# Mixture-of-experts tail of an attention kernel: tokens and expert weights turned by DMA, last projection in quarters, reordered experts

## The chip, the cores and the metric

The kernel runs on one core of one Trainium2 chip. The time is device microseconds (us) for one execution. A core has TensorE (PE), VectorE (DVE), ScalarE (ACT), GpSimd (POOL) and SyncE (SP), which here issues every DMA. Each engine works through its own list of instructions in order and waits on semaphores for the others.

## The reference

```python
h = layernorm(x)                          # x: 8 sequences x 128 tokens x 256
q, k, v = h @ wq, h @ wk, h @ wv          # 16 query heads, 4 key/value heads of 128
q, k = rope(rms_norm(q)), rope(rms_norm(k))
k_ctx, v_ctx = rms_norm(ctx @ wk_ctx), ctx @ wv_ctx
p = softmax(q @ [k_ctx; k].T / sqrt(128) + causal)
x = x + (p @ [v_ctx; v]) @ wo
t = layernorm(x)                          # 1024 tokens x 256
score = sigmoid(t @ gate.T)               # 8 experts, the two best by score + bias
for e in range(8):                        # bf16 products
    xe = bf16(t * score_of_e_or_0)
    out += (silu(xe @ w1[e].T) * (xe @ w3[e].T)) @ w2[e].T
out += (silu(t @ sh_w1.T) * (t @ sh_w3.T)) @ sh_w2.T
x = x + out
```

The shapes are fixed: 8 sequences of 128 tokens, model width 256, expert width 128, context of 128 rows for each sequence.

## The kernel before

The attention part runs sequence by sequence. A "row" is one sequence `b`, and each row has four groups `g` of four query heads. Rows 0 and 7 are written out and rows 1 to 6 are a loop. Within a row PE computes the scores, turns the query of the next group and the probabilities (`turn_probs`), mixes the values (`mix`), and projects the queries two groups ahead. The output projection `out_proj(b - 1)` (L1314) of 48 matmuls into `proj[0]` stands in the next row. The matmuls are done on split high and low parts, so ACT makes a high part (`o_copy`, `p_copy`, all through the helper at L435) and DVE the low part (`o_low`, `p_low`, at L879).

After row 7 comes the mixture of experts. The 1024 tokens are two halves `n` of four tiles of 128 tokens, and step `k` of 16 is expert `k % 8` on half `k // 8`. The order of all instructions is written out by hand.

- The weights of the experts are loaded in rows 0 to 3, cast to bf16 by POOL (L815, the signals `w1_cast`, `w3_cast`, `w2_cast`), and turned by PE in `turn_experts` (L1328): six groups of eight 128x128 transposes into PSUM, copied to SBUF by ACT or DVE (`turned`). The shared expert's weights are turned as four fp32 transposes (L1447).
- The normalised tokens `xn2_all` are turned in pairs of tiles (`turn_xn2`, L1346) and copied to `xn2T` (`xn_copy`). The router is `logits` (L1355) on PE, `gate_exp` on ACT (L622) and ten small DVE instructions (`router`, L1077), which end in `weight`.
- For each step `k`, DVE scales two of the four token tiles by `weight` and POOL the other two (`e_scale`, L1102 and L825) into `xb`, which has two buffers. PE turns the eight blocks (`turn_tokens`, L1458, line L1469) into `turn` or `o_ps`, and ACT copies them to `xbT` (`e_copy`). `expert_up` (L1473, L1481) makes the two hidden products, ACT the SiLU (`e_act`, L647), DVE the product (`e_hidden`, L1115), and `expert_down` (L1485, L1488) adds into `proj`. Steps k and k + 1 use two sets of PSUM banks, so `expert_up(k)` waits for `e_hidden(k - 2)`, and PE runs `expert_up(k + 1)` ahead of `expert_down(k)`.
- The shared expert is `shared_up` (L1493, L1501), a SiLU (L655), a product (L1134) and `shared_down` (L1505), which first clears the two banks with a product with zeros (L1512) and then makes eight passes of fp32 matmuls (L1516).
- PE's order around the tail: `logits(0)`, `turn_probs(8, 0)`, shared weights, w3, tokens of tiles 4 and 5, the last `mix`, w2, the whole of `out_proj(7)`, `shared_up(0)`, `turn_xn2(3)`, `turn_tokens(0)`, `logits(1)`, and only then the experts.
- DVE after row 7: the low parts, the ten instructions of `router(0)`, a weight copy (L979), `e_scale(0)` and `e_scale(1)`, then `residual(7)` (L961) and `second_norm(7)` (L972), whose root POOL makes between its own `e_scale` instructions (`l2_root`, L714).
- SP's list: the loads, `next_ctx(b)` (L408: the context of the next sequence, as soon as its buffer is free), w3 after `w1_cast` (L417), w2 after `w3_cast` (L420), and the four stores of the output (L427).

## Time and profile before

| | |
|---|---|
| time, median of 3 runs | 376.64 us (376.41 to 376.70) |
| time of the profiled execution | 377.97 us |
| its span, first to last instruction | 376.3 us |
| PE busy | 343.7 us, 91% |
| DVE busy | 325.6 us, 87% |
| ACT busy | 271.2 us, 72% |
| POOL busy | 165.8 us, 44% |
| mean granted clock of PE | 0.977 |

The span is what the trace covers; the time of an execution lies a little above it. Busy shares are averages over stages with different limits, and overlapped matmuls count as busy. PE's clock is given as a share of its full 2.4 GHz. Of the span, roughly the last 60 us belong to the mixture of experts, with the output projection of row 7 among them.

### The profile page before, as it was taken

Reading aid. Unit: us, or ns where it says so; the run is one execution under the profiler, and the core shown is the slowest. Engines: PE = TensorE matmul, PEld = TensorE weight load, DVE = VectorE, ACT = ScalarE, POOL = GpSimd, SP = SyncE. Lnnn points to the kernel's source line nnn. Section 1 sums busy time; section 2 is a strip of 40 time slices with the busy share of each in tenths; the row PEclk is TensorE's granted clock in tenths of the full one; section 3 lists DMA queues with packets and bytes.
Section 4 is the critical chain, followed back from the end, with each engine's and each line's share of the span. In section 5 each row is a group of like instructions: output and inputs, shape, how many; then the busy total and the mean of one; then the engine's idle time right before and its main releaser. Section 6 shows DMA issues by size and latency. Waiting matters only on the chain.

```text
span 376.3 us, 7781 instructions
## 1 busy us (share of the span) xinstructions
PE 343.7 (91%) x2471; PEld 237.3 (63%) x2476; DVE 325.6 (87%) x625; ACT 271.2 (72%) x913; POOL 165.8 (44%) x242
## 2 busy tenths in 40 slices
PE   6697798799999999999999999999999999998994
PEld 5373555376567665866685577567666778674572
DVE  1668999998999899899989998999899897759653
ACT  3557879676986797699759876986797567167562
POOL 3356565652754275427344443644174300334330
PEclk9788989999999999999999999999999999989999
DMA  5967000000030003000000000000000000000011
GB/s 179 379 212 223 17 0 2 1 2 14 3 111 0 14 0 111 14 1 0 0 14 0 0 0 14 0 0 0 0 0 1 2 0 2 2 0 3 22 35 57
DMA packets 11603, 13.49 MB, mean 36 GB/s; under 512 B 824, under 2 KB 9024, under 8 KB 11584
## 3 DMA queue, kind: packets, MB, share of 16 engines
q1 hardware_dynamic: 11584, 13.25, 11.0%
q8 instruction: 10, 0.16, 0.2%
q14 instruction: 9, 0.07, 0.1%
HBM read 12.20 MB, written 1.05 MB: 35 GB/s over the span
## 4 chain that ended last, share of the span: by engine, by line
PE 40%; DVE 24%; ACT 17%; issue 10%; POOL 4%; DMA 2%; SPq 1%; DVEq 1%; ACTq 0%; POOLq 0%
PE proj L1324 10%; ACT probs L524 8%; PE pt_ps L1300 5%; DVE probs L953 5%; PE proj L1157 4%; PE turn L1246 3%; DVE nmax L941 3%; DVE pT_lo L879 3%; PE o_ps L1310 3%; POOL q_rot L744 3%; PE sc_ps L1267 2%; ACT pT_hi L435 2%; DMA wq<-in_L_xattn_wq_dram 2%; ACT q_junk L468 2%; DVE q_t L870 2%
## 5 line engine op out<-in xcount | busy, mean ns | idle before, releaser
L524 ACT ACTIVATE probs<-sc_ps,nbias,q_r 128x256 f32<-128x256 f32 x128 | 70.8, 574 | 2.8 <-DVE nbias L945 2.8
L744 POOL TENSOR_TENSOR q_rot<-q_t 128x512 f32<-128x512 f32 x32 | 41.4, 1295 | 42.8 <-DVE q_t L872 42.0
L953 DVE TENSOR_SCALAR probs<-probs,rden 128x256 f32<-128x256 f32 x128 | 51.2, 461 | 1.1
L1157 PE MATMUL proj<-wq_hi,xT 128*128 128x512 f16 x128 | 40.1, 396 | 2.9 <-DVE wq_lo L863 2.9
L435 ACT ACTIVATE pT_hi<-pt_ps 128x512 f16<-128x512 f32 x64 | 34.8, 597 | 10.9 <-PE pt_ps L1300 10.9
L468 ACT ACTIVATE q_junk<-proj 128x128 bf16<-128x128 f32 x128 | 34.0, 295 | 11.7 <-DVE q_t L872 11.7
L879 DVE SCALAR_TENSOR_TENSOR pT_lo<-pt_ps,pT_hi 128x512 f16<-128x512 f32 x64 | 41.0, 682 | 0.6 <-ACT pT_hi L435 0.6
L941 DVE TENSOR_REDUCE nmax<-sc_ps 128x4 f32<-128x1024 f32 x32 | 38.9, 1214 | 1.5 <-PE sc_ps L1289 1.5
L831 POOL TENSOR_TENSOR wq<-xn_all,weight 128x512 bf16<-128x512 f32 x16 | 17.1, 1074 | 44.1 <-DVE weight L1098 23.4
L1324 PE MATMUL proj<-wo_hi,oT_hi 128*128 128x256 f16 x128 | 34.9, 273 | 0.0
L1324 PE MATMUL proj<-wo_lo,oT_hi 128*128 128x256 f16 x128 | 34.9, 273 | 0.0
L1324 PE MATMUL proj<-wo_hi,oT_lo 128*128 128x256 f16 x128 | 34.9, 273 | 0.0
L1300 PE MATMUL pt_ps<-ident,probs 128*128 128x128 f32 x256 | 34.2, 278 | 0.3
L701 POOL TENSOR_TENSOR q_r<-q_me,power 128x4 f32<-128x4 f32 x32 | 33.3, 1042 | 2.5
L435 ACT ACTIVATE qT_hi<-turn 128x512 f16<-128x512 f32 x32 | 19.5, 610 | 19.9 <-PE turn L1246 19.9
L1300 PEld LDWEIGHTS pt_ps<-ident,probs 128*128 128x128 f32 x256 | 29.5, 143 | 0.8 <-DVE probs L953 0.5
L1246 PE MATMUL turn<-ident,q_rot 128*128 128x128 f32 x128 | 19.8, 277 | 10.6 <-POOL q_rot L744 4.9
L468 ACT ACTIVATION_READ_ACCUMULATOR q_junk<-proj 128x1 f32 x128 | 28.5, 227 | 0.0
L524 ACT ACTIVATION_READ_ACCUMULATOR probs<-sc_ps,nbias,q_r 128x1 f32 x128 | 27.6, 215 | 0.0
L1310 PE MATMUL o_ps<-pT_hi,v_hi 128*128 128x512 f16 x64 | 24.3, 379 | 3.2 <-DVE pT_lo L879 3.2
L879 DVE SCALAR_TENSOR_TENSOR oT_lo<-o_ps,oT_hi 128x512 f16<-128x512 f32 x32 | 21.9, 686 | 5.8 <-ACT oT_hi L435 5.8
L1267 PE MATMUL sc_ps<-kT_hi,qT_hi 128*128 128x256 f16 x128 | 24.5, 273 | 0.5 <-ACT probs L524 0.2
(216 smaller groups left out, 920.7 us busy)
## 6 DMA issues: line engine op xcount, KB each, us to landing
wq<-in_L_xattn_wq_dram SPq DMA_DIRECT2D x4, 512.0 KB, 9.1
w<-in_L_ffn_w_dram SPq DMA_DIRECT2D x2, 1024.0 KB, 10.5
wq<-in_L_xattn_wo_dram SPq DMA_DIRECT2D x1, 2048.0 KB, 8.2
ctx_b<-in_ctx_dram SPq DMA_DIRECT2D x8, 128.0 KB, 2.1
out_dram<-x_all SPq DMA_DIRECT2D x4, 256.0 KB, 2.2
x_all<-in_x_dram SPq DMA_DIRECT2D x1, 896.0 KB, 12.3
wkc<-in_L_xattn_wk_ctx_dram SPq DMA_DIRECT2D x1, 512.0 KB, 4.2
wk<-in_L_xattn_wk_dram SPq DMA_DIRECT2D x1, 512.0 KB, 5.1
```

The lines of the kernel that those rows point to most:

```text
L435: return nc.scalar.activation(out_, in_, ACT.Copy, scale=scale)
L468: last = nc.scalar.activation(junk[:, head], bank[:, head], ACT.Square, scale=scale, accum_out=dst[:, h:h + 1])
L524: last = nc.scalar.activation(probs[:, h, :], sc_ps[:, h, :], ACT.Exp, bias=nbias[:, h:h + 1], scale=q_r[:, g, h:h + 1], accum_out=den[:, ...
L701: nc.gpsimd.tensor_tensor(r, me, power[:], ALU.pow).then_inc(root, 1)
L744: nc.gpsimd.tensor_tensor(q_rot[:], q_t1[:], q_t2[:], ALU.add).then_inc(q_added, 1)
L879: return nc.vector.scalar_tensor_tensor(out=lo, in0=src, scalar=scale, in1=hi, op0=ALU.mult, op1=ALU.subtract)
L941: nc.vector.tensor_reduce(nmax[:], sc_ps[:], AX_X, ALU.max, negate=True).then_inc(s_max, 1)
L953: last = nc.vector.tensor_scalar(probs[:, h, :], probs[:, h, :], rden[:, h:h + 1], None, ALU.mult)
L1157: last = nc.tensor.matmul(bank[:], xT[:, a, c, :], w[:, c, cols], start=(n == 0), stop=(n == 3 * DC - 1))
L1300: last = nc.tensor.transpose(pt_ps[:, a, h * P:(h + 1) * P], probs[:, h, a * P:(a + 1) * P], ident[:])
L1310: last = nc.tensor.matmul(o_ps[:], v[:, a, g * P:(g + 1) * P], p[:, a, :], start=(a == 0 and i == 0), stop=(a == 1 and i == 2))
L1324: last = nc.tensor.matmul(proj[0][:, 0:D], o[:, h // R, (h % R) * P:(h % R + 1) * P], w[:, h, :], start=(h == 0 and i == 0), stop=(h == H ...
```

## The change

1. The expert weights are turned by six DMAs of SP (`dma_start_transpose`, 256 KB each) in rows 1 to 4 in place of PE's 48 transposes and their six copies.
2. The scaled tokens are turned by one such DMA for each step `k` (256 KB, from SBUF to SBUF) in place of eight PE transposes and ACT's copy. The buffers are four (`xb`) and six (`xbT`). Of the four tiles ACT now scales one, DVE one and POOL two. DVE and ACT scale five steps ahead (`LEAD`).
3. `out_proj(7)` is cut in quarters by group; three run ahead of the last low part.
4. `logits(0)` goes into row 7, and the shared weights are turned there. DVE's `router(0)` goes around the last `p_low` and ahead of the last `o_low`. Two copies in row 7 and that of tiles 4 and 5 go from DVE to ACT.
5. `logits(1)`, its exponential and `router(1)` come after the first half's experts have begun.
6. The clearing products (L1512) go; the first shared product into each bank starts it.

```diff
--- before.py
+++ after.py
...
         hid_s = spare[:, 512:1024]
         silu_e = spare[:, 1024:2048].rearrange("p (a t) -> p a t", a=2)
-        xbT = spare[:, 2048:3072].bitcast(BF16).rearrange("p (a c t) -> p a c t", a=2, c=DC)
-        xb = spare[:, 3072:4096].bitcast(BF16).rearrange("p (a t d) -> p a t d", a=2, t=TT)
+        xb_homes = (spare[:, 3072:3584], spare[:, 3584:4096], k_sum[:], k_rot[:])
+        xbT_homes = (spare[:, 2048:2560], spare[:, 2560:3072], k_t1[:], k_t2[:], kc_n[:], q_t1[:])
+        xb = [h.bitcast(BF16).rearrange("p (c t d) -> p c t d", c=DC, t=TT) for h in xb_homes]
+        xbT = [h.bitcast(BF16).rearrange("p (c t) -> p c t", c=DC) for h in xbT_homes]
+        NB, NX = len(xb), len(xbT)
+        LEAD = 5
...
+        def token_turned(eng, k):
+            eng.wait_ge(d_xbT[k % NX], 16 * (k // NX + 1))
...
@@ -411,16 +414,38 @@
+            def turn_up(dst, src):
+                for half in half_e:
+                    sp.dma_start_transpose(dst[:, half].rearrange("p e c n -> p (e c) n"),
+                                           src[:, half].rearrange("p e d -> p (e d)")).then_inc(d_wT, 16)
+            def turn_down():
+                for half in half_e:
+                    sp.dma_start_transpose(w2T[:, half].rearrange("p e (c q) -> p (e c) q", c=DC),
+                                           w2_b[:, half].rearrange("p e c n -> p (e c n)")).then_inc(d_wT, 16)
             next_ctx(2)
             next_ctx(3)
             sp.wait_ge(w1_cast, 4)
             sp.dma_start(w1_32[:], w3.rearrange("e h d -> h e d")).then_inc(d_w3, 16)
+            turn_up(w1T, w1_b)
             next_ctx(4)
             sp.wait_ge(w3_cast, 4)
             sp.dma_start(w1_32[:].rearrange("p e (c h) -> p (e c) h", c=DC),
                          w2.rearrange("e (c p) h -> p (e c) h", p=P)).then_inc(d_w2, 16)
-            with sp.Fori(5, B) as b:
+            turn_up(w3T, w3_b)
+            next_ctx(5)
+            sp.wait_ge(w2_cast, 4)
+            turn_down()
+            with sp.Fori(6, B) as b:
                 next_ctx(b)
+            for k in range(E * NT):
+                for scaled in (e_scaled, e_scaled2, e_scaled3):
+                    sp.wait_ge(scaled, k + 1)
+                seen(sp, e_up, k - NX + 1)
+                sp.dma_start_transpose(xbT[k % NX].rearrange("p c (t n) -> p (c t) n", t=TT),
+                                       xb[k % NB].rearrange("p c t d -> p (c t d)")).then_inc(d_xbT[k % NX], 16)
             with sp.Fori(0, B // 2) as i:
                 sp.wait_ge(y_added, i + 1)
...
+                    if g == 2 and last:
+                        act.wait_ge(t_sh2, 1)
+                        copy(gateT[:].rearrange("p c e -> p (c e)"), proj[0][:, D:D + DC * E])
+                        copy(sh2T[:], proj[0][:, 0:D]).then_inc(r_sh2, 1)
+                        xn_copy(1)
                     if g == 0:
...
-            turned(w1T[:, half_e[0]], proj[0][:].bitcast(BF16), t_w1a, r_w1a)
-            gate_exp(0)
-            p_copy(G * B - 1)
-            turned(sh13T[:], turn[:], t_sh13, r_sh13, "p a c n -> p (a c n)")
-            turned(w3T[:, half_e[0]], proj[0][:].bitcast(BF16), t_w3a, r_w3a)
-            o_copy(G * B - 1, G - 1)
-            turned(w2T[:, half_e[0]], pt_ps[:, 0, :].bitcast(BF16), t_w2a, r_w2a, "p e n -> p (e n)")
...
+            def e_scale(k):
+                act.wait_ge(g_weight, k // E + 1)
+                if k >= NB:
+                    token_turned(act, k - NB)
+                dst, src, w = tile_of(k, 0)
+                copy(dst, src, w).then_inc(e_scaled3, 1)
...
-            xn_copy(3)
-            e_copy(0)
-            gate_exp(1)
+            o_copy(G * B - 2, G - 2)
+            gate_exp(0)
+            turned(sh13T[:], turn[:], t_sh13, r_sh13, "p a c n -> p (a c n)")
+            xn_copy(2)
+            p_copy(G * B - 1)
+            o_copy(G * B - 1, G - 1)
+            for k in range(LEAD):
+                e_scale(k)
             for n in range(NT):
                 act.wait_ge(sh_up, n + 1)
                 seen(act, sh_hid, n)
                 nc.scalar.activation(silu_s, shared_banks(n)[0], ACT.Silu).then_inc(sh_silu, 1)
                 if n == 0:
-                    e_copy(1)
+                    xn_copy(3)
                 e_act(E * n)
-                e_copy(E * n + 2)
+                if n == 0:
+                    e_act(1)
+                    gate_exp(1)
                 for k in range(E * n, E * (n + 1)):
-                    if k + 1 < E * (n + 1):
+                    if k + 1 < E * (n + 1) and k:
                         e_act(k + 1)
-                    if k + 3 < E * (n + 1) + (2 if n + 1 < NT else 0):
-                        e_copy(k + 3)
+                    if k + LEAD < E * NT:
+                        e_scale(k + LEAD)
...
-            e_scale(0)
-            e_scale(1)
+            for k in range(3):
+                e_scale(k)
             l2_root(B - 1)
-            for k in range(2, E):
+            for k in range(3, E):
                 e_scale(k)
...
-            p_low(G * B - 1)
-            turned(w3T[:, half_e[1]], proj[1][:].bitcast(BF16), t_w3b, r_w3b)
-            xn_copy(2)
-            o_low(G * B - 1, G - 1)
...
-            for part in range(4):
-                router(0, part)
-            turned(w2T[:, half_e[1]], sc_a.bitcast(BF16), t_w2b, r_w2b, "p e n -> p (e n)")
+            router(0, 0)
+            router(0, 1)
+            p_low(G * B - 1)
+            router(0, 2)
+            router(0, 3)
+            o_low(G * B - 1, G - 1)
             e_scale(0)
             e_scale(1)
             residual(B - 1)
+            e_scale(2)
             second_norm(B - 1)
-            e_scale(2)
+            e_scale(3)
+            e_scale(4)
...
-                if n == 0:
-                    e_scale(3)
                 for k in range(E * n, E * (n + 1)):
                     e_hidden(k)
-                    if k < 4:
+                    if k == 1:
+                        router(1, 0)
+                    if 1 <= k < 4:
                         router(1, k)
-                    if k + 4 < E * NT:
-                        e_scale(k + 4)
+                    if k + LEAD < E * NT:
+                        e_scale(k + LEAD)
...
+            def out_quarter(g):
+                if g == 0:
+                    pe.wait_ge(wo_low2, 1)
+                    pe.wait_ge(wo_low, 2)
+                    pe.wait_ge(r_sh2, 1)
+                pe.wait_ge(o_ready, G * (B - 1) + g + 1)
+                for h in range(g * R, (g + 1) * R):
+                    for i, (o, w) in enumerate(((oT_hi, wo_hi), (oT_hi, wo_lo), (oT_lo, wo_hi))):
+                        last = nc.tensor.matmul(proj[0][:, 0:D], o[:, g, (h % R) * P:(h % R + 1) * P], w[:, h, :],
+                                                start=(h == 0 and i == 0), stop=(h == H - 1 and i == 2))
...
                     if g == 2 and last:
                         turn_down_gate()
                         turn_xn2(0, (q_sq, G * B))
+                        turn_xn2(1, (q_ready, G * B))
                     if g == 3 and last:
-                        turn_xn2(1, (q_ready, G * B))
-                        pe.wait_ge(w1_cast, 4)
                         pe.wait_ge(r_sh2, 1)
-                        turn_experts(proj[0][:], w1_b, 0, False, t_w1a)
-                        pe.wait_ge(n_ready[0], 1)
-                        turn_experts(proj[1][:], w1_b, 1, False, t_w1b)
+                        logits(0)
+                        turn_shared()
...
-            logits(0)
+            turn_xn2(2, (s_exp, U))
+            out_quarter(0)
             turn_probs(B, 0)
...
-            turn_experts(proj[0][:], w3_b, 0, False, t_w3a)
-            pe.wait_ge(r_w1b, 1)
-            turn_experts(proj[1][:], w3_b, 1, False, t_w3b)
-            turn_xn2(2, (s_exp, U))
+            out_quarter(1)
             mix(U - 1, G - 1)
...
+            out_quarter(2)
+            out_quarter(3)
...
+            shared_up(0)
+            turn_xn2(3, (r_sh13, 1))
+            pe.wait_ge(d_wT, wT_landed)
             pe.wait_ge(n_ready[2], 1)
-            turn_experts(sc_a, w2_b, 1, True, t_w2b)
-            pe.wait_ge(r_w3a, 1)
-            out_proj(B - 1)
-            shared_up(0)
-            turn_xn2(3, (r_w2b, 1))
-            turn_tokens(0)
-            logits(1)
-            pe.wait_ge(r_w2a, 1)
             for n in range(NT):
                 expert_up(E * n)
-                if n == 0:
-                    turn_tokens(1)
-                turn_tokens(E * n + 2)
                 shared_down(n)
                 for k in range(E * n, E * (n + 1)):
                     if k + 1 < E * (n + 1):
                         expert_up(k + 1)
-                    if k + 3 < E * (n + 1) + (2 if n + 1 < NT else 0):
-                        turn_tokens(k + 3)
-                    if k + 1 == E * (n + 1) and n + 1 < NT:
+                    elif n + 1 < NT:
                         shared_up(n + 1)
+                    if k == 0:
+                        logits(1)
                     expert_down(k)
...
```

## Rows read from the trace of the kernel before

**Rows 1.** First line of the page: the profiled span.
```profile
span 376.3 us, 7781 instructions
```

**Rows 2.** Chain of waits, 316 to 371 us: start us, us, what.
```profile
316.27 1.31 PE o_ps L1310 x6
...
322.62 2.24 DVE wq L1108 x4
...
330.97 0.38 PE sc_ps L1481
...
351.08 1.72 PE sc_ps L1501 x4
...
360.67 0.43 PE sc_ps L1481 x2
...
361.53 0.45 PE turn L1469 x8
361.98 0.44 PE proj L1488 x4
...
369.86 0.60 ACT wq L647
```

**Rows 3.** PE in order of time: start us, us, what.
```profile
318.30 0.27 PE L1324 MATMUL proj<-wo_hi,oT_hi 128*128 128x256 f16 x1
...
323.54 1.88 PE L1501 MATMUL sc_ps<-xn2T,sh13T 128*128 128x512 f32 x4
...
327.57 0.63 PE L1351 MATMUL sc_ps<-ident,xn_all 128*128 128x128 f32 x4 [0.43 <-DVE xn_all L974]
...
328.97 1.92 PE L1360 MATMUL o_ps<-gateT,xn2T 128*128 128x8 f32 x16 [0.33 <-ACT xn2T L435]
...
354.35 0.60 PE L1488 MATMUL proj<-w2T,wk 128*128 128x256 bf16 x4
...
360.07 0.60 PE L1488 MATMUL proj<-w2T,wk 128*128 128x256 bf16 x4
...
361.81 0.60 PE L1488 MATMUL proj<-w2T,wk 128*128 128x256 bf16 x4
...
371.23 0.61 PE L1488 MATMUL proj<-w2T,wk 128*128 128x256 bf16 x4 [0.69 <-DVE wk L1115]
```

**Rows 4.** Groups by shape, 300 to 377 us: busy us, mean ns.
```profile
L831 POOL TENSOR_TENSOR wq<-xn_all,weight 128x512 bf16<-128x512 f32 x16 | 17.1, 1074 | 44.1 <-DVE weight L1098 23.4 <-PE o_ps L1469 12.2 <-PE turn L1469 8.5
...
L1115 DVE TENSOR_TENSOR wk<-pt_ps,wq 128x512 bf16<-128x512 f32 x16 | 11.0, 687 | 8.0 <-ACT wq L647 8.0
```

**Rows 5.** Windows of 1 us; PEclk follows POOL's column.
```profile
331.00:332.00 1.00, 1.00 (x7) 0.60 (x7) 0.00 (x0) 0.98 (x2) 0.00 (x0) 0.78 0.00 0
332.00:333.00 1.00, 1.00 (x12) 1.00 (x11) 0.00 (x0) 0.99 (x3) 0.13 (x1) 0.50 0.00 0
...
334.00:335.00 1.00, 1.00 (x4) 0.81 (x3) 1.00 (x2) 1.00 (x2) 0.96 (x1) 0.52 0.00 0
```

**Rows 6.** DVE, then ACT, in order of time.
```profile
339.64 1.40 DVE L1108 TENSOR_SCALAR wq<-xn_all,weight 128x256 bf16<-128x256 f32 x2
...
331.15 1.28 ACT L655 ACT_TABLE_LOAD   x1
332.44 0.60 ACT L655 ACTIVATE wq<-sc_ps 128x512 f32<-128x512 f32 x1
```

**Rows 7.** Page, DMA issues: KB each, median us to landing.
```profile
wq<-in_L_xattn_wo_dram SPq DMA_DIRECT2D x1, 2048.0 KB, 8.2
ctx_b<-in_ctx_dram SPq DMA_DIRECT2D x8, 128.0 KB, 2.1
out_dram<-x_all SPq DMA_DIRECT2D x4, 256.0 KB, 2.2
```

**Rows 8.** SP's queue in order of time.
```profile
107.03 0.38 SPq L417 DMA_DIRECT2D w<-in_L_ffn_w_dram  x1
121.62 0.33 SPq L410 DMA_DIRECT2D ctx_b<-in_ctx_dram  x1
```

More of the change, by code:

```diff
@@ L222, in xattn_moe_kernel @@
         d_w2 = sem("d_w2")
+        d_wT = sem("d_wT")
         d_sh = sem("d_sh")
@@ L1043, in row @@
                         wo_split(1)
-                    if g == 3 and last:
-                        turned(w1T[:, half_e[1]], proj[1][:].bitcast(BF16), t_w1b, r_w1b)
                     if g == 2 and not last:
@@ L1326, in out_proj @@
                 last.then_inc(wo_done, 1)
-            def turn_experts(bank, src, half, per_chunk, signal):
-                for j in range(8):
-                    e, c = half * (E // 2) + j // DC, j % DC
-                    one = src[:, e, c, :] if per_chunk else src[:, e, c * P:(c + 1) * P]
-                    last = nc.tensor.transpose(bank.bitcast(BF16)[:, j * P:(j + 1) * P], one, identb[:])
-                last.then_inc(signal, 1)
             def turn_down_gate():
@@ L1344, in turn_down_gate, with turn_shared @@
                 last.then_inc(t_sh2, 1)
+            def turn_shared():
+                for a, src in enumerate((sh1, sh3)):
+                    for c in range(DC):
+                        last = nc.tensor.transpose(turn[:, (a * DC + c) * P:(a * DC + c + 1) * P],
+                                                   src[:, c * P:(c + 1) * P], ident[:])
+                last.then_inc(t_sh13, 1)
             def turn_xn2(i, free):
```

114 lines of the change are left out of this document (31 added, 83 removed).

## The prediction

> **What bounds the kernel now.** The span of the profiled execution is 376.3 us [rows 1]. It ran in 377.97 us, 1.67 more, and the median of the runs shown is 376.64, 0.34 above the span. I make the sum on the span and add 0.34. The edit leaves rows 0 to 6 alone but for SP's list, so I read the chain of waits and PE's order from 316 us on. The reader should see three stretches there. First, the last `mix`, begun at 316.27 [rows 2], is followed by the whole of `out_proj(7)`, from 318.30 to 323.54 [rows 3]: 48 matmuls in 5.24 us, 1.31 a quarter. Second, up to the first expert product at 330.97 [rows 2] stand `shared_up(0)` (two groups of 1.72 [rows 2]), a wait of DVE and POOL for the norm of tile 7, its transposes at 327.57 and `logits(1)` of 1.92 [rows 3]. Third, the experts run with PE as the bound: in the second half `expert_down` begins at 360.07 and 361.81 [rows 3], a step of 1.75 us that is 0.87 for `expert_up` (two of 0.43), 0.45 for the token transposes and 0.44 for `expert_down` [rows 2]. The clock fell to half (1.2 of 2.4 GHz) as these began [rows 5].
>
> **Weights by DMA.** PE loses six groups of eight transposes, of which the token group has the price, 0.45 [rows 2], so 2.7 us; two such groups (0.9) stand between the last `mix` and the projection. The six copies on ACT and DVE go with them. On SP each pair of DMAs stands ahead of `next_ctx`. Between SP's issues at 107.03 and 121.62 [rows 8] there are 14 us, and the context is wanted a row later still, so two DMAs of even 4 us cost nothing. If they took over 7 us each, SP would begin to run late, and the transpose DMA would be lost for the tokens long before that.
>
> **Last projection in quarters.** Ahead of the last `mix`, PE loses four groups of eight (1.8) and tiles 2 and 3 (0.44, now in group 2, under a wait of PE for `p_low`), and gains two quarters (2.6); `logits(0)` and the shared weights only swap places. The last `mix` thus comes some 0.3 later. Its low part was ready at 316.27 + 1.31 + 0.60 (ACT) + 0.69 (DVE) = 318.9 [rows 2, 4], and will be at 319.3 with the signals; the third quarter and two parts of DVE's router (1.6) fill the time. The last quarter ends at 319.3 + 1.31 = 320.7, against 323.54. Gain 2.8. Who waits for the moved router: `e_scale(0)`, by less than it gains, since `weight` comes at 318.7 and not 322.0.
>
> **Up to the first expert.** `shared_up(0)` ends at 324.15. The norm of tile 7 took 3.9 us from the end of the projection, with two `e_scale` of DVE (2.24 [rows 2]) in front. Now it has the same two, held up by POOL: DVE's scaling of two tiles at 339.64 took 1.40 [rows 6], at a time when POOL was in its own, against 1.12 for two in the run of four (2.24) of which half lay beside POOL, so DVE's SBUF work stands until POOL's instruction is over. POOL has a third `e_scale` of 1.07 [rows 4] ahead of its root. I take 4.4 us, so 325.1, and 0.45 of transposes: the first expert product begins at 325.6 instead of 330.97. That is 5.4 gained in all; 0.5 less if POOL delays DVE twice, 0.9 more if it never does. `turn_tokens(0)` and `logits(1)` are no longer in front.
>
> **First half.** Before, from 330.97 to the start of `expert_down(7)` at 354.35 [rows 3], 23.4 us. After: 8 x 0.87 + 7 x 0.44 + 1.8 (`shared_down`, without clearing) + 1.9 (`logits(1)`) + 3.44 (`shared_up(1)`) = 17.2 us of PE at the full clock. Waits come on top. PE ends `expert_up(0)` at 326.4, but DVE's `e_scale(3)` and `e_scale(4)`, each held until POOL is through with its own, end at 327.1 and the shared product (0.69) at 327.8: `shared_down(0)` waits 1.4. ACT is no later: `e_scale(4)` waits for the first token DMA (323.6), then 0.4, the load of SiLU's table 1.28 [rows 6] and the SiLU 0.6 make 325.9. Behind `e_act(1)` stands the router's exponential: with SiLU on both sides it needs up to two more loads, 2.6, and behind it are queued ACT's `e_scale(5)` and `e_act(2)`; on DVE, `router(1)` waits for it, ahead of `e_hidden(2)`. From the end of `expert_up(1)`: ACT ends `e_act(2)` after 0.6 + 1.28 + 0.2 + 0.4 + 1.28 + 0.5 = 4.3, DVE ends `e_hidden(2)` after 5.2; PE has 1.9 + 0.44 + 0.87 + 0.44 + 0.87 = 4.5 of work until it wants that. So the two loads cost 0.7, not 2.6, and the router's rest in DVE another 1.2 in steps 3 to 6. If the exponential is in SiLU's table the loads cost nothing and 0.3 comes back. Sum 17.2 + 1.4 + 1.9 = 20.5, gain 2.9. The tile that ACT now scales shows nowhere; I take 0.4, between DVE's 0.56 a tile (2.24 for four) and half of a SiLU of 0.60 over twice the columns [rows 2]; either end fits in a step of 1.31.
>
> The trace has the SiLU at 332.44, directly behind the load that began at 331.15 [rows 6]. The Trainium skill (ScalarE: Activation LUTs, What ACT_TABLE_LOAD costs) has 1.28 us too, but counts a drain of 1.38 for each switch to another set. By its figures `e_act(2)` would come 2.8 later and the time would be 371.4.
>
> **Clock.** In four windows from 331 to 335 the granted clock was 0.78, 0.50, 0.50 and 0.52 [rows 5] (the window at 333 is as that at 332), which took 1.7 us of full speed. It fell after PE had idled 0.43 and 0.33 us [rows 3] and then run `logits(1)` with 8 columns a product. The new order has longer waits (1.0 before the last tokens' transposes, 1.4 before `shared_down(0)`) and the same 8 columns behind them, so I count 1.7 again: the first half then gains 1.2.
>
> **Second half.** Steps lose five token groups after `shared_down(1)`, 2.25 us. PE's work is then 1.31 a step, but the two PSUM sets make a loop: `expert_up` to `expert_down` of one step is SiLU 0.60 [rows 2] + product 0.69 [rows 4] + signals, 1.5, so two steps take 1.31 + 1.5, 1.4 each. Six steps give back 0.8. Ahead of `shared_down(1)` the clearing product (0.4) goes, but its wait for DVE's two sums stays and DVE's shared product follows them: nothing. Gain 1.4. POOL's 1.07 a step [rows 4] fits.
>
> **Token DMA.** Sixteen DMAs of 256 KB on one queue. The trace has none of this kind. From below: the load of 2048 KB in 8.2 [rows 7] is 1.0 us for 256 KB. From above: two contexts of 128 KB at 2.1 each, one after the other, 4.2. A store of 256 KB landed in 2.2 [rows 7]. I take a pace of 1.5 and a landing 3 us after issue, near the store. The first is issued at 320.2 and wanted at 325.6. With a pace up to 2 nothing waits beyond what is counted; at 2.5 the span grows by 2 to 4, as the tokens of steps 13 to 15 come late.
>
> The Trainium skill has two answers. Advanced Engine Details and Errata (X-Bar Transpose (TRN2)) says that transpose DMAs are as fast as others, which agrees with my choice. VectorE: DVE Perf Modes (The three transpose paths) gives 1309 ns for one 128x128 block by DMA and advises TensorE where PSUM will do; eight such blocks one after the other would be 10.5 us a step and put the kernel beyond 480 us. No row here shows either.
>
> **Sum.** 376.3 - 2.8 - 2.6 - (2.9 - 1.7) - 1.4 = 368.3 by these rounded terms; with the median's 0.34, 368.6.
>
> **Rivals.**
> - The clock holds. For it: 3.4 us of full work (`shared_up(0)`) come right before. Against: the longer waits. The time is 1.7 less, 366.9. Chance 0.18.
> - Tokens land late: a pace of 2.2 to 3 us, or other waits between the engines (POOL holding up DVE, a second fall of the clock). Between the bounds above it is well possible. 371 to 376, say 373. Chance 0.10.
> - A switch of ACT's table costs more than its load. If each of the two new ones held ACT for as long again as the load, 2.6 us, all of it would be on the path, since PE already waits for `e_hidden(2)`: 371.2. Against it stands the SiLU right behind its load. Chance 0.04. (The skill's drain is this rival.)
> - Slower: the DMA's pace becomes the bound of all sixteen steps. The last token must land by 368.8, when `expert_up(15)` stood before, to be no slower: 320.2 + 3 + 15 x pace = 368.8 gives 3.04 us. At 4.2, the upper bound, it lands at 386.2, 17 us worse: 394. For it: no row shows data turned on the way, and each DMA here is small. Against: plain transfers of this size are below 3 us. It decides from a pace of 3.04 us, 86 GB/s. Chance 0.20. (The skill's figure for single blocks is this rival.)
> - The change doesn't do what it says: SP's three waits and the four buffers hold the scaling back so that PE waits as long as it turned before, and nothing moves. At a step of 1.75 in both halves and the first expert still behind the norm, 376.6. Chance 0.03.
>
> **Chances.** Forecast 0.45. Faster by over 0.2% (about what a measurement of this kernel can tell from no change): 0.45 + 0.18 + 0.10 + 0.04 = 0.77; same 0.03; slower 0.20. The range is 365.0 to 377.0: below by the norm that POOL never delays (0.9), a clock that holds (1.7) and a table that serves both functions (0.3), with 0.7 for my rounding; above by everything but the slow DMA.
>
> **What would show it.** The last L1324 quarter's matmuls ending near 320.7. The first L1481 product near 325.6. Three loads of ACT's table after 320 us in place of one. A clock of 0.5 for some 3 to 4 us soon after `logits(1)`. Steps of 1.3 to 1.45 in the second half, with `expert_up` released by DVE. DMA transposes landing less than 2 us apart. Wrong would be waits of L1481 for a DMA, SP busy for over 2 us an issue, or contexts landing late in rows 2 to 5.

## The result, and the profile after

| | before | after |
|---|---|---|
| median of four executions on one chip | 376.52 us (374.57 to 376.70) | 366.07 us (364.95 to 366.59) |
| span of the profiled execution | 376.3 us [rows 1] | 364.3 us (it ran in 366.01) |
| mean granted clock of PE | 0.977 | 0.989 |

The ratio is 0.9736, with a 95% interval of 0.9709 to 0.9763: the kernel is 2.6% faster, 2.5 us more than forecast and inside the range. The head of the page after, and PEclk in 40 slices:

```profile
span 364.3 us, 7426 instructions
...
PEclk9899989999999999999999999999999999999999
```

The change did what it says: 22 DMA transposes appear, and with them the packets under 512 B rise from 824 to 24056 by the pages. PE in order of time, after (start us, us, engine, line, operation, out<-in, count, and in brackets the idle time before and what ended it):

```profile
298.76 1.04 PE L1315 MATMUL pt_ps<-ident,probs 128*128 128x128 f32 x8
...
317.49 0.27 PE L1338 MATMUL proj<-wo_hi,oT_lo 128*128 128x256 f16 x1
317.60 1.88 PE L1503 MATMUL sc_ps<-xn2T,sh13T 128*128 128x512 f32 x4
...
321.31 0.63 PE L1378 MATMUL turn<-ident,xn_all 128*128 128x128 f32 x4
321.77 0.59 PE L1483 MATMUL sc_ps<-wq,w1T 128*128 128x512 bf16 x2
...
324.01 1.97 PE L1515 MATMUL proj<-sh2T,wq 128*128 128x256 f32 x8 [1.21 <-DVE wq L1149]
...
326.67 1.85 PE L1387 MATMUL o_ps<-gateT,xn2T 128*128 128x8 f32 x16
...
332.06 0.61 PE L1490 MATMUL proj<-w2T,wk 128*128 128x256 bf16 x4 [0.93 <-DVE wk L1129]
...
337.35 0.61 PE L1483 MATMUL sc_ps<-wq,w1T 128*128 128x512 bf16 x2 [1.35 <-DMA wq<-k_sum]
...
343.68 0.60 PE L1490 MATMUL proj<-w2T,wk 128*128 128x256 bf16 x4
...
356.37 0.61 PE L1490 MATMUL proj<-w2T,wk 128*128 128x256 bf16 x4
357.82 0.61 PE L1490 MATMUL proj<-w2T,wk 128*128 128x256 bf16 x4
359.26 0.61 PE L1490 MATMUL proj<-w2T,wk 128*128 128x256 bf16 x4 [0.82 <-DVE wk L1129]
```

The first row is `turn_probs(7, 1)`, 8 transposes that open the tail in every kernel here. In the trace of before it began at 301.77:

```profile
301.77 1.04 PE L1300 MATMUL pt_ps<-ident,probs 128*128 128x128 f32 x8
```

The order of work ahead of it is the same but for SP's list and one POOL `memset`, yet its start differs between the twelve traces (298.50 to 301.77), and between the two of one kernel (301.77 and 300.83 before, 298.76 and 300.33 after). Where I looked, the granted clock of the first 50 us differed too: in the window from 28 to 32 us it was 0.90 before and 1.00 after, from 44 to 48 us 1.00 and 0.67. So I compare the tail from that row on. The table gives each mark as time after it. The kernel after was run and traced a second time, as was the kernel before.

| us after the start of `turn_probs(7, 1)` | before | before, again | forecast | after | after, again |
|---|---|---|---|---|---|
| last matmul of the last projection begins | 21.66 | 21.66 | 18.9 | 18.73 | 18.74 |
| first expert product begins | 29.20 | 29.34 | 23.8 | 23.01 | 23.03 |
| `expert_down(7)` begins | 52.58 | 52.58 | 46.0 | 44.92 | 44.19 |
| last `expert_down` begins | 69.46 | 69.47 | 61.5 | 60.50 | 59.78 |

The tail gained 9.0 and 9.7 us against a forecast of 8.0. After the last `expert_down` both kernels need another 5.0 to 5.2 us. The rest of the 12.0 us between the two spans is the start: 3.0 in this pair, but 0.5 between the two repeats (300.83 and 300.33). The start moves by 0.9 and 1.6 us between two executions of one kernel, so whether the change moves it at all is open.

DVE after, from its `e_scale(0)` and `e_scale(1)` to the shared product, and below it POOL in the same stretch (columns as above):

```profile
316.14 1.51 DVE L1124 TENSOR_SCALAR wq<-xn_all,weight 128x256 bf16<-128x256 f32 x2
317.80 0.42 DVE L992 SCALAR_TENSOR_TENSOR x_all<-proj,x_all 128x256 f32<-128x256 f32 x1
...
320.04 1.12 DVE L1003 TENSOR_SCALAR xn_all<-x_all,ln_mv,ln_rs 128x256 f32<-128x256 f32 x1 [0.76 <-POOL ln_rs L722]
321.08 1.13 DVE L1124 TENSOR_SCALAR k_rot<-xn_all,weight 128x256 bf16<-128x256 f32 x1
322.13 1.13 DVE L1124 TENSOR_SCALAR wq<-xn_all,weight 128x256 bf16<-128x256 f32 x1
323.18 0.68 DVE L1149 TENSOR_TENSOR wq<-pt_ps,wq 128x512 f32<-128x512 f32 x1
```

```profile
319.97 1.04 POOL L859 TENSOR_TENSOR k_rot<-xn_all,weight 128x512 bf16<-128x512 f32 x1
320.97 2.14 POOL L859 TENSOR_TENSOR wq<-xn_all,weight 128x512 bf16<-128x512 f32 x2
```

Three DVE instructions take 1.12 or 1.13 us each. The first, the norm's scaling, takes 0.41 with POOL at rest (experiment 5), and an `e_scale` of DVE alone takes 0.32 to 0.35. The first ends at 321.16 and the last at 323.26, both 0.15 behind the end of a POOL `e_scale` (321.01, 323.11). That chain, and not PE, decides when `shared_down(0)` may begin.

ACT after, its three table loads and what follows each:

```profile
320.47 1.28 ACT L681 ACT_TABLE_LOAD   x1
321.76 0.60 ACT L681 ACTIVATE wq<-sc_ps 128x512 f32<-128x512 f32 x1
...
327.49 1.28 ACT L654 ACT_TABLE_LOAD   x1
328.78 0.20 ACT L654 ACTIVATE r_exp<-o_ps 128x32 f32<-128x32 f32 x1
...
329.39 1.28 ACT L668 ACT_TABLE_LOAD   x1
330.69 0.60 ACT L668 ACTIVATE wq<-sc_ps 128x512 f32<-128x512 f32 x1
```

SP's queue after (the time is how long the issuing instructions held SP), and the page's list of DMA issues (count, median us from issue to landing):

```profile
104.48 5.00 SPq L419 DMA_TRANSPOSE w1T<-w_b  x2
...
316.63 2.63 SPq L447 DMA_TRANSPOSE wq<-wq  x2
...
331.83 1.24 SPq L447 DMA_TRANSPOSE wq<-k_sum  x1
```

```profile
wq<-wq SPq DMA_TRANSPOSE x4, 3.3
w1T<-w_b SPq DMA_TRANSPOSE x2, 5.4
...
wq<-k_sum SPq DMA_TRANSPOSE x1, 5.5
wq<-k_rot SPq DMA_TRANSPOSE x1, 5.1
```

A transpose of 256 KB mostly holds SP for 1.23 to 1.34 us (that of step 7 held it for 2.54), where the issue of a plain DMA held it for 0.33 to 0.38 [rows 8], and by the page's medians it lands 3.0 to 3.4 us after issue, where a store of the same size took 2.2 [rows 7]. Two of the sixteen token DMAs, those of steps 6 and 7, landed late, after 5.5 and 5.1 us.

### The profile page after: what moved, and what is told of

It reads as the page before. It is cut to its first block, busy times and chain, and to the rows that moved or that the text cites. A ratio compares the mean times of both kernels' runs of the same rounds, so it can differ in the third digit from the quotient of the medians.

```text
span 364.3 us, 7426 instructions
## 1 busy us (share of the span) xinstructions
PE 329.9 (91%) x2296; PEld 223.4 (61%) x2296; DVE 316.9 (87%) x602; ACT 263.7 (72%) x916; POOL 166.5 (46%) x241
## 2 busy tenths in 40 slices
DMA packets 34835, 19.25 MB, mean 53 GB/s; under 512 B 24056, under 2 KB 32256, under 8 KB 34816
## 3 DMA queue, kind: packets, MB, share of 16 engines
q1 hardware_dynamic: 34816, 19.02, 20.6%
## 4 chain that ended last, share of the span: by engine, by line
PE 35%; DVE 24%; ACT 18%; issue 10%; POOL 6%; DMA 3%; SPq 1%; DVEq 1%; ACTq 0%; POOLq 0%
PE proj L1352 10%; ACT probs L549 7%; DVE probs L982 5%; PE pt_ps L1315 5%; PE turn L1261 3%; DVE nmax L970 3%; POOL q_rot L772 3%; PE o_ps L1325 3%; DVE pT_lo L908 3%; PE proj L1172 3%; PE sc_ps L1282 3%; ACT pT_hi L460 2%; DVE q_t L899 2%; ACT kc_junk L493 2%; DMA wq<-in_L_xattn_wq_dram 2%
## 5 line engine op out<-in xcount | busy, mean ns | idle before, releaser
L772 POOL TENSOR_TENSOR q_rot<-q_t 128x512 f32<-128x512 f32 x32 | 42.4, 1325 | 41.3 <-DVE q_t L901 40.5
L1172 PE MATMUL proj<-wq_hi,xT 128*128 128x512 f16 x128 | 39.2, 389 | 2.1 <-DVE wq_lo L892 2.1
L460 ACT ACTIVATE qT_hi<-turn 128x512 f16<-128x512 f32 x32 | 19.5, 610 | 20.5 <-PE turn L1261 20.5
L1352 PE MATMUL proj<-wo_hi,oT_hi 128*128 128x256 f16 x112 | 30.5, 273 | 0.0
L1352 PE MATMUL proj<-wo_lo,oT_hi 128*128 128x256 f16 x112 | 30.5, 273 | 0.0
L1352 PE MATMUL proj<-wo_hi,oT_lo 128*128 128x256 f16 x112 | 30.5, 273 | 0.0
L460 ACT ACTIVATE oT_hi<-o_ps 128x512 f16<-128x512 f32 x32 | 19.6, 613 | 7.8 <-PE o_ps L1325 7.8
```

Of the source, the lines that this page charges most:

```text
L460: return nc.scalar.activation(out_, in_, ACT.Copy, scale=scale)
L772: nc.gpsimd.tensor_tensor(q_rot[:], q_t1[:], q_t2[:], ALU.add).then_inc(q_added, 1)
L1172: last = nc.tensor.matmul(bank[:], xT[:, a, c, :], w[:, c, cols], start=(n == 0), stop=(n == 3 * DC - 1))
L1352: last = nc.tensor.matmul(proj[0][:, 0:D], o[:, h // R, (h % R) * P:(h % R + 1) * P], w[:, h, :], start=(h == 0 and i == 0), stop=(h == H ...
```

## The experiments

My theory: the gain comes from PE's path in four places, as in the table, and the token DMAs stay hidden. The rivals: the DMA's pace is near its limit; the clock and not the removed work explains the surplus; the quarters bring nothing of their own. Every ratio is to the kernel before on the same chip in the same session. Its median was 376.16 us for experiments 1 to 3, 376.56 for 5 to 7 and the repeat of the changed kernel, and 377.29 for 4, so the ratios compare more safely than the times. "Changed kernel" means its second run, 366.58 us, ratio 0.9739.

**1. The DMA's pace, two and three times.** Each token DMA is preceded by one or two more that turn the same data into memory no longer in use, and the consumers count all of them.

```diff
-            eng.wait_ge(d_xbT[k % NX], 16 * (k // NX + 1))
+            eng.wait_ge(d_xbT[k % NX], 32 * (k // NX + 1))
...
+                for i in range(1):
+                    sp.dma_start_transpose(again[i * NX + k % NX]...,
+                                           xb[k % NB]...).then_inc(d_xbT[k % NX], 16)
                 sp.dma_start_transpose(xbT[k % NX]...
```

> The changed kernel with each of the 16 token DMAs issued twice in a row (the extra one writes to unused memory, and the step waits for both), so that a step takes two issues of SP, 2.6 us in place of 1.3. Nothing of the result is left out. Theory A (the token DMAs are hidden up to a pace of about 2 us, the bound is PE and the loop of PSUM banks): the first tokens still land before they are wanted, the last ones late; 3 to 6 us slower than the changed kernel, 369 to 372 us. Theory B (the landing of the tokens already sets the pace of the changed kernel, as the one wait of 1.4 us at step 6 suggests): every step pays, 16 x 1.3 = 20 us, 386 us.

> As before with each token DMA issued three times: 3.9 us a step, beyond the point of 3.04 us from which the prediction called the change slower than the old kernel. Theory A: the DMA is then the bound of all steps; the last token lands at 317 + 3 + 15 x 3.9 = 378 us of the span and the end follows some 7 us later, 383 to 392 us, slower than before the change by 2 to 4%. If the buffers or other waits had hidden more, it would stay below 377.

Measured: with two 377.46 us, ratio 1.0018 (0.9993 to 1.0043); with three 398.64 us in two executions, ratio 1.0586 (1.0517 to 1.0656). SP's queue with two, then some of the waits of its PE from 316 us on (us in total, times, longest):

```profile
316.42 1.26 SPq L455 DMA_TRANSPOSE w<-wq  x1
317.73 1.33 SPq L457 DMA_TRANSPOSE wq<-wq  x1
319.17 1.26 SPq L455 DMA_TRANSPOSE w<-wq  x1
```

```profile
PE sc_ps L1493 <- DMA k_t<-k_rot: 2.4, 1, 2.4
```

A step costs 2.75 us with SP issuing for 2.59 of them (316.42 to 319.17), and 4.14 with three. PE waited for seven of the sixteen tokens, 9.6 us in all, and the whole gain was gone: slower than theory A allows, faster than B. With three it waited 24 us, and the time overshot what was expected. Most of that is the pace: over the fifteen steps from the first real token DMA (319.38) to the last (382.73) it was 4.22 and not 3.9, which makes 4.8 us, and the first one came 2.4 later than assumed. The clock also stood at 0.50 to 0.62 in three stretches of 4 to 12 us, but behind the first two PE caught up and was waiting for tokens again. So the slower rival's mechanism is real, and its place, the last `expert_up`, is right. Its point of decision was put at a pace of 3.04; the real tokens of the doubled kernel were issued from 317.73 to 360.82, 2.87 apart, and the last `expert_up` began at 365.37, which is 66.9 after `turn_probs(7, 1)` against 67.0 before. The limit is thus about 2.9, and the changed kernel, at 1.31, is far from it.

**2. The second router's logits ahead of the experts again.** `logits(1)`, its copy and its exponential go back to where before had them; all else is the changed kernel.

```diff
             pe.wait_ge(n_ready[2], 1)
+            logits(1)
             for n in range(NT):
...
                     elif n + 1 < NT:
                         shared_up(n + 1)
-                    if k == 0:
-                        logits(1)
                     expert_down(k)
```

> The changed kernel with logits(1) and its exponential back ahead of the experts, so that one load of the SiLU table follows the last exponential and the two further loads are gone. Theory A: 1.9 us of logits and a wait of 0.6 for the copy of xn2 come ahead of the first expert, SiLU and the shared product come 3 us later, and 1.9 us of PE work and about 0.9 of waiting at steps 2 and 3 go: 0 to 1 us slower, 366 to 367 us. Theory B (the two table loads of 1.28 us, or more with a drain, are all on the path): 1 to 3 us faster, 363 to 365 us.

Measured: 370.64 us, ratio 0.9843 (0.9806 to 0.9881), 4.1 above the changed kernel (3.9 by the ratios) and against both expectations. Its PE:

```profile
324.44 1.92 PE L1386 MATMUL o_ps<-gateT,xn2T 128*128 128x8 f32 x16 [0.78 <-ACT xn2T L460]
...
329.38 3.75 PE L1514 MATMUL proj<-sh2T,wq 128*128 128x256 f32 x8 [1.41 <-DVE wq L1148]
332.92 0.74 PE L1482 MATMUL sc_ps<-wq,w1T 128*128 128x512 bf16 x2
...
337.99 0.61 PE L1489 MATMUL proj<-w2T,wk 128*128 128x256 bf16 x4 [1.01 <-DVE wk L1128]
```

Windows of 4 us, first of this kernel, then of the changed kernel (PE, PEld, DVE, ACT and POOL busy with instructions, then PEclk, DMA share, GB/s):

```profile
324.00:328.00 4.00, 3.41 (x19) 2.20 (x20) 0.98 (x1) 1.87 (x4) 2.57 (x3) 0.80 0.68 131
328.00:332.00 4.00, 2.62 (x6) 2.19 (x7) 1.55 (x3) 1.00 (x2) 0.35 (x1) 0.50 0.00 0
```

```profile
324.00:328.00 4.00, 3.99 (x25) 3.32 (x25) 1.22 (x3) 1.11 (x2) 1.20 (x2) 1.00 0.55 102
328.00:332.00 4.00, 3.14 (x21) 1.83 (x20) 2.72 (x9) 3.96 (x7) 0.00 (x0) 1.00 0.34 65
```

The first expert comes 3.0 us later (26.0 against 23.03 after `turn_probs(7, 1)`), 2.04 from the start of `logits(1)` to it, and 0.95 more between the last transposes and the logits, 0.78 of it the wait for ACT's copy; behind the logits the clock falls to 0.50, as it did in before [rows 5], and `shared_down(0)` takes 3.54 us instead of 1.80. The tail is 3.5 longer in all (63.24 against 59.78), though this trace has no wait for a late token and the other has 0.72 of them. So the placement of one router costs at least 3.5 us here, and 1.7 of it can be pinned on the clock, by what `shared_down(0)` took longer. In the changed kernel the same 8-column products come with `shared_down(0)` and an `expert_up` directly before them and an `expert_down` directly behind.

The two loads of ACT's table that this edit takes out from between the experts brought nothing back: PE still waited for DVE at `expert_down(2)`, 1.01 us (last row of the PE fence) against 0.93. Between the products of steps 1 and 2 DVE ran five instructions of `router(1)` and an `e_scale` (335.37 to 337.25).

And the clock doesn't need these products to fall. With three DMAs it went to 0.50 before any of them had run in that stretch, behind waits of 1.14 and 2.21 us:

```profile
326.11 3.75 PE L1525 MATMUL proj<-sh2T,wq 128*128 128x256 f32 x8 [2.21 <-DVE wq L1159]
```

There `logits(1)` came only at 331.36. Later in that trace waits of 1.79 and 2.61 passed at full clock, and it was down again from 349 us on, behind one of 3.38. So what is shown is that the router's place decides it in this kernel; which part of the place does (the columns, the wait, or what runs before and behind) is not.

**3. The quarters undone.** All four quarters stand behind the last `mix`.

```diff
-            out_quarter(0)
             turn_probs(B, 0)
-            out_quarter(1)
             mix(U - 1, G - 1)
-            out_quarter(2)
-            out_quarter(3)
+            for g in range(G):
+                out_quarter(g)
```

> The changed kernel with the four quarters of the last projection together behind the last mix, as the old kernel has them. Theory A: three quarters of 1.31 us no longer run while DVE and ACT make the last low part; the projection ends 2.5 to 2.9 us later and all that follows too, 368.6 to 369.0 us. Theory B (the norm of tile 7 is set by POOL's own scaling, not by the end of the projection): at most 1 us slower, since POOL has finished its three scalings when the projection ends.

Measured: 367.79 us, ratio 0.9759 (0.9720 to 0.9799). The interval overlaps that of the changed kernel (0.9700 to 0.9779), so the trace must decide; it is of the slowest of the four executions (370.24), so I go by its marks and not by its length. In it the last projection ends 2.2 us later (20.96 against 18.74) and the first expert comes 2.4 later (25.45 against 23.03); at the last `expert_down` it is 3.1, of which 1.1 is a longer wait (1.7 us against 0.6) for the token DMA of step 7. PE now waits 1.81 us for the last low part, which the quarters had filled. So the quarters do carry a gain of their own, 2.2 in the trace; on the median only 1.2 of it shows, less than was expected.

**4. Only the weights by DMA**, on the kernel before: PE's six groups and their copies go, the six DMAs come, and nothing else moves. (The edit deletes the calls of `turn_experts` and `turned` for w1, w3 and w2 and adds the SP lines of the change for the weights.)

> The kernel before with only its 48 expert weight transposes on PE and their six copies replaced by the six DMAs of the change. Theory A: of the 2.7 us of PE work only the 0.9 between the last mix and the last projection lies on the path, with 0.6 of DVE's last copy; the rest was under waits for the probabilities: 0.8 to 1.5 us faster than the kernel before, 374.9 to 375.6 us. Theory B (PE is the bound all along): 2.7 us faster, 373.7 us. Theory C (SP's transposes hold up the contexts): slower.

Measured: 376.35 us, ratio 0.9978 (0.9953 to 1.0003): no difference that shows. Theory B, 2.7 us, is outside the interval; the median lies 0.9 below, which theory A would allow, but the trace shows only 0.1. Its DVE, then its POOL:

```profile
319.81 2.81 DVE L1119 TENSOR_SCALAR wq<-xn_all,weight 128x256 bf16<-128x256 f32 x4
322.55 0.41 DVE L976 SCALAR_TENSOR_TENSOR x_all<-proj,x_all 128x256 f32<-128x256 f32 x1
```

```profile
319.86 2.09 POOL L844 TENSOR_TENSOR wq<-xn_all,weight 128x512 bf16<-128x512 f32 x2 [21.08 <-DVE weight L1109]
```

Counted from `turn_probs(7, 1)` (299.64) its projection ends 1.0 earlier (20.65 against 21.66), but the residual behind it begins at 22.91 and the first expert at 29.09, against 23.02 and 29.20 before. DVE's router and four `e_scale` of 2.81, held up by POOL, stand between. PE's time came free in a place where DVE ends last. In the changed kernel DVE is out of the way: the row that makes `weight` stands 16.4 after `turn_probs(7, 1)` (315.14), here 20.0 (319.59). That comes from the router's new place (point 4 of the change) and not from the quarters, for with the quarters undone (experiment 3) it stands at 16.3, and there DVE waits for PE's projection:

```profile
316.91 0.19 DVE L1115 SCALAR_TENSOR_TENSOR weight<-rank,score 128x32 f32<-128x32 f32 x1
...
321.92 0.42 DVE L992 SCALAR_TENSOR_TENSOR x_all<-proj,x_all 128x256 f32<-128x256 f32 x1 [2.49 <-PE proj L1338]
```

What the removal is worth inside the change is not shown: no run has the change with the expert weights still on PE.

**5. DVE's order behind the norm.** `e_scale(3)` and `e_scale(4)` of DVE go behind the shared product, ACT's `e_scale(4)` behind its first SiLU, and POOL waits for the norm before its step 3.

```diff
             second_norm(B - 1)
-            e_scale(3)
-            e_scale(4)
...
             l2_root(B - 1)
+            pool.wait_ge(l2_done, B)
             for k in range(3, E):
                 e_scale(k)
-            pool.wait_ge(l2_done, B)
...
+                if n == 0:
+                    e_scale(3)
                 for k in range(E * n, E * (n + 1)):
                     e_hidden(k)
+                    if k == 0:
+                        e_scale(4)
```

> The changed kernel with three waits taken out by order: DVE scales steps 3 and 4 behind the first shared product, ACT scales step 4 behind the first SiLU (so that the load of its table waits for no DMA), and POOL begins step 3 only when the norm of tile 7 is done. Theory A (POOL's instruction holds up DVE's SBUF instructions, and the shared product behind two of them is what PE waits for): the norm ends 0.7 us earlier, shared_down(0) starts at 322.6 instead of 324.0, all later work too: 1.2 to 1.6 us faster than the changed kernel, 364.4 to 364.9 us. Theory B (the wait is passed on to steps 2 to 4, where ACT's tables and the router are late): within 0.4 us.

Measured: 365.59 us, ratio 0.9703 (0.9675 to 0.9732), 1.0 below the changed kernel; the intervals overlap, so the trace must say what moved. Its DVE:

```profile
321.65 0.41 DVE L1004 TENSOR_SCALAR xn_all<-x_all,ln_mv,ln_rs 128x256 f32<-128x256 f32 x1 [0.76 <-POOL ln_rs L723]
323.48 0.69 DVE L1148 TENSOR_TENSOR wq<-pt_ps,wq 128x512 f32<-128x512 f32 x1 [1.42 <-ACT wq L681]
```

With POOL at rest the norm's scaling takes 0.41 instead of 1.12, and PE's wait ahead of `shared_down(0)` falls from 1.21 to 0.20 us. `shared_down(0)` begins 1.3 earlier (23.95 against 25.26), and the tail is 1.2 shorter (58.56 against 59.78). The same meeting of DVE and POOL comes back later, though: DVE's `e_scale` at 334.68 takes 1.23 beside one of POOL that begins at 334.72, and `expert_down(4)` waits 0.94 us for DVE, where in the changed kernel PE idled about 0.2. Without the 0.72 of late tokens that only the other trace has, the gain would be about 0.5.

**6. A third pair of banks in the second half.** `turn` and `o_ps` no longer hold tokens, so three steps can be in flight there, and `expert_up(9)` runs ahead of `shared_down(1)`. (PE's waits are changed to match; the lines are left out below.)

```diff
+            if k >= E:
+                return (up_pairs + ((turn[:], o_ps[:]),))[(2, 1, 0)[(k - E) % 3]]
             return up_pairs[(k + k // E) % 2]
...
-                    if k + 1 < E * (n + 1):
-                        expert_up(k + 1)
+                    if k + 1 + n < E * (n + 1):
+                        expert_up(k + 1 + n)
```

> The changed kernel with a third pair of PSUM banks (turn and o_ps, free there) for the experts of the second half, and expert_up two steps ahead of expert_down; expert_up(9) then runs ahead of shared_down(1). Theory A (steps of the second half are set by the loop expert_up, SiLU, product, expert_down over two pairs, 1.44 us, and not by PE's 1.31 or by the DMA): steps of 1.31 us and 0.87 of PE work under the wait of 1.2 for the shared product: 1.3 to 1.7 us faster, 364.3 to 364.8 us. Theory B (the token DMAs or the scaling set the pace): within 0.3 us.

Measured: 365.99 us, ratio 0.9729 (0.9700 to 0.9758), 0.6 below the changed kernel, which the intervals don't separate. Its PE:

```profile
349.08 0.59 PE L1489 MATMUL turn<-q_t,w1T 128*128 128x512 bf16 x2
...
351.68 0.59 PE L1489 MATMUL sc_ps<-wq,w1T 128*128 128x512 bf16 x2
...
353.58 0.60 PE L1489 MATMUL turn<-k_t,w1T 128*128 128x512 bf16 x2 [0.43 <-DMA k_t<-k_sum]
```

These two are two steps apart, 1.30 us each, PE's bare work, where the changed kernel needs 1.44 to 1.45 (356.37, 357.82, 359.26). From the first to the last `expert_up` of that half the trace is 1.6 shorter, as theory A says; the 0.6 of the medians doesn't settle it. At step 14 PE is fast enough to wait 0.43 us for its token: here the DMAs become the next bound.

**7. Both.**

> Both edits together. If the two waits are independent the gains add: 2.5 to 3.2 us faster than the changed kernel, 362.9 to 363.5 us. If the DMA of the tokens becomes the bound as PE gets faster (its pace of 1.31 us is that of PE's work), less than 2 us.

Measured: 364.65 us, ratio 0.9676 (0.9638 to 0.9715), the lowest median of all, 1.9 below the changed kernel, with intervals that still touch. That is less than the sum of the two expectations: besides the waits of 0.44 us at step 14 and 0.36 at step 6 for token DMAs, the wait of 0.95 at `expert_down(4)` that came with DVE's new order is there too. The tail is no shorter than with the third pair alone (57.53 against 57.41).

**8. Each kernel once more.** The two repeats of the table.

> The changed kernel again, unedited, beside the next three: it gives their base on this chip, 365.5 to 366.6 us, and tells whether two things of its first trace come back: the landing of the token DMA of step 6 after 5.5 us where the others took 3.1 to 3.4, with a wait of PE of 1.4 us (theory A: chance, so it is elsewhere or absent; theory B: it is tied to that step), and a start of row 7 some 3 us earlier than in the trace of the kernel before (theory A: PE's clock in the first 50 us varies between executions of either kernel; theory B: it belongs to the change).

> The kernel before again, unedited, for a second trace of it. Theory A (PE's clock over the first 50 us is a matter of the execution): its last row starts up to 3 us earlier or later than in the first trace, with a different pattern of low clock before 52 us. Theory B (the start belongs to the kernel): its last row starts within 0.3 us of the first trace, 3 us behind the changed kernel's. In both, the clock falls to 0.5 at the first experts again.

Measured: the changed kernel 366.58 us, ratio 0.9739 (0.9700 to 0.9779); the kernel before 377.03 us in one execution. In this second trace of before `turn_probs(7, 1)` started 0.9 us earlier than in the first, in that of the changed kernel 1.6 later, with another pattern of low clock ahead of it, so the start is a matter of the execution at least in good part. The clock fell as the experts began in both traces of before (0.73 and 0.84 from 328 to 336 us in the repeat) and in neither of after. The late landings came back in after, at steps 6 and 7 (4.3 and 4.9 us), with waits of 0.15 and 0.57 us in place of 1.35. They appear in some kernels with the same DMAs (5.4 and 5.0 in the one with both edits, 3.3 and 5.8 with the quarters undone) and not in others (3.3 and 3.6 with DVE's new order, 3.0 and 3.2 with the logits ahead). With doubled DMAs steps 5 and 6 had them.

One thing goes with them in the traces. The profile counts, beside SP's DMAs, a queue of instructions (q8, single packets of 0.02 MB; the time of one comes to about 0.9 to 1.6 us of one DMA engine). In the changed kernel such a packet came at 333.0, while the DMAs of steps 6 and 7 (issued at 331.83 and 333.25) were on the way. The same holds in its repeat (334.6), with both edits (333.2), with doubled DMAs (334.5, steps 5 and 6), with three (349.9, step 7, 4.4 and 4.9 us) and with the quarters undone (339.4, when step 7's was on the way, 5.8 us; step 8's, issued 0.4 behind the packet's start, took 4.2). With DVE's new order it came at 329.5, as one token DMA landed and 0.3 before the next was issued, and with the third pair of banks at 330.8, within 0.2 us of an issue, and nothing was late; with the logits ahead it came 0.7 us behind the issue of step 8, which landed after 3.8. That is a coincidence seen in these traces and not a tested cause; no run here was made for it.

## Why the prediction was right, and where it was off

**Last projection: right.** Forecast 2.8 us, measured 2.9. Undoing the quarters gives back 2.2. Undoing everything but the weights' DMAs leaves 1.0 at this mark and 0.1 behind DVE. So the quarters carry most of the gain, and the removal of PE's groups on its own none that reaches the first expert.

**Up to the first expert: right in kind, the norm mis-sized.** Forecast 2.6, measured 3.3. I took 4.4 us from the projection's end to the tokens' last transposes. It took 3.7 (317.60 to 321.31). I had put two `e_scale` of DVE behind the projection; both were done as it ended (316.14 to 317.65), and the residual began 0.2 us behind the start of `shared_up(0)`. POOL did hold up DVE's scaling for the norm, 1.12 in place of 0.41, and experiment 5 shows that by taking POOL away.

**First half: the step that failed is the clock.** I counted 1.7 us for a second fall to half clock. It didn't fall: every window of 4 us from 312 to 340 shows 1.00. The 20.5 us of the full-clock sum were then right to a tenth: from the first expert to `expert_down(7)` the trace has 21.91 us, of which 1.35 is the wait for the late token of step 6, and the repeat 21.16 with 0.72 of such waits, so 20.6 and 20.4. My argument was that longer waits with 8-column products behind them would bring the clock down as before. The longer waits came (1.21 and 0.93) and the clock stood. Experiment 2 puts the same products ahead of the experts again, and there it fell. What before and this experiment share is the order: `shared_up(0)`, the token transposes, a short idle stretch (0.33 and 0.78 us) for ACT's copy, the logits, then the experts. The rival "the clock holds" came true: I had given it a chance of 0.18 and 366.9 us, and the measured 366.07 is nearer to that than to the forecast. Waits can bring the clock down here: experiment 1 shows it behind 1.14 and 2.21 us. Those of 1.21 and 0.93 did not.

**Inside the first half.** `shared_down(0)` waited 1.21 for the shared product (forecast 1.4), and PE waited 0.93 at `expert_down(2)`, where I had put 0.7 for the two extra table loads. Their share of it is not shown: DVE's product waited 0.33 us for the SiLU behind the third load, but experiment 2, without these loads, has the wait too (1.01), behind the router on DVE. The loads numbered three, at 1.28 us each. The exponential and both SiLUs began 0.01 to 0.02 us behind their loads, so the rival with a dearer switch of tables fell. By the Trainium skill (ScalarE: Activation LUTs, What ACT_TABLE_LOAD costs) each switch also has a drain of 1.38 us; the rows show none, and the measurement decides.

**Second half: right.** Forecast 1.4 us, measured 1.3 (16.88 to 15.58 and 15.59). The step is 1.44 to 1.45 us at its end, the loop over two bank pairs as worked out, and experiment 6 brings it to 1.30 by a third pair.

**Token DMA: hidden, with a price that I got half right.** The pace was taken as 1.5 us and is 1.31, set by how long an issue holds SP; the landing was taken as 3 and is 3.0 to 3.4. What I had not in the sum is the late landing, 0.7 to 1.35 us on PE's path. The rival that these DMAs bound everything needed a pace of 3.04; experiment 1 built it, and the limit is about 2.9. The two answers of the Trainium skill can now be weighed. That transposes by DMA are as fast as others (Advanced Engine Details and Errata, X-Bar Transpose (TRN2)) holds for the order of size only: 3.3 us against 2.2 for the store. That one 128x128 block costs 1309 ns (VectorE: DVE Perf Modes, The three transpose paths) doesn't add up block by block: eight blocks in one DMA have a pace of 1.31 us.

**The weights' DMAs: free.** They held SP for 2.5 to 2.7 us each beside a load of 1 MB and 1.3 otherwise, and the contexts behind them were issued at 118.64 and 154.16 us with no wait that a row shows. The 4 us each that I allowed were ample.

**The sum.** Projection 2.9, first expert 3.3, first half 1.5 to 2.2, second half 1.3: 9.0 to 9.7 against 8.0. The medians differ by 10.4 and 10.0; the rest, 1.4 and 0.3 us, is not in the tail, and the start, which varies by more than that between executions of one kernel, does not explain it. Part of the closeness is luck: the late landings, which were not in my sum, took back 1.35 and 0.72 of what the clock gave. Without them the tail would have gained 10.3 and 10.4.

## What to carry to other kernels

Work taken off the busiest engine is worth what the next chain lets through: the removed weight transposes gave nothing alone (experiment 4), because DVE's router and scaling ended last there. Look for that chain first. When a DMA takes the place of an engine, double it on the chip: that shows in one run how far its pace is from becoming the bound, and where. And look at what stands around products with few columns: in this kernel, one router's place was worth 3.5 us, 1.7 of them clock.

## What the runs showed of the hardware that was not expected

- A DMA transpose of 256 KB from SBUF to SBUF mostly held SP for 1.23 to 1.34 us (2.54 in one), four times an ordinary issue (0.33), and back to back SP's issue sets the pace: 2.75 us for two, 4.14 for three.
- Such a DMA landed in 3.0 to 3.4 us, in 5.0 to 5.4 beside a load of 1 MB, and now and then in 4.3 to 5.8; in the first half each of these had a packet of an instruction queue while it was on the way.
- A scaling of DVE from SBUF to SBUF that met one of POOL's lasted until 0.15 us behind POOL's end: 0.41 became 1.12, and 0.34 twice became 1.13. One that had begun 0.10 us ahead of POOL's (334.38 against 334.48) kept its 0.35; one that had begun 0.04 ahead (experiment 5) did not.
- The clock stayed at its full level through waits of 1.21 and 1.35 us between the experts and fell behind one of 0.78 us that the logits followed. It also fell without the logits, behind waits of 1.14 and 2.21 us (three DMAs).
